# Cross-attention of the second layer: dividing by the softmax sum before the output projection, and projecting once per batch row instead of once per pair of heads

## What is computed

```python
x = x + tanh(g_xattn[0]) * xattn0(layernorm(x), ctx)     # 16 heads of 16
x = x + tanh(g_ffn[0])   * moe(layernorm(x))             # 16 experts
x = x + tanh(g_xattn[1]) * xattn1(layernorm(x), ctx)     # 16 heads of 128
x = x + tanh(g_ffn[1])   * ternary_ffn(layernorm(x))

def xattn1(t, c):                                        # the part that is changed
    q = (t @ Wq), k = (c @ Wk), v = (c @ Wv)             # two heads share a k and a v
    attn = softmax(mask(q @ k.T / sqrt(128)))            # (4, 16, 256, 1601)
    return (attn @ v).reshape(4, 256, 2048) @ Wo
```

## Time and profile before

| | us |
|---|---|
| median of 3 runs | 1572.19 (1567.17 to 1576.84) |
| the profiled execution | 1572.19, span of its instructions 1570.9 |
| mean granted TensorE clock in it | 0.962 of full speed |

### The profile page before, as it was taken

One profiled execution on the slowest core, in us unless ns is written; L12 is line 12 of the kernel. 1 busy time (PEld: TensorE's weight loads), 2 busy tenths in 40 slices (PEclk: granted clock), 3 DMA queues, 4 the chain that ended last, 5 costly groups with the idle time before them and its releaser, 6 DMA issues.

```text
span 1570.9 us, 25673 instructions
## 1 busy us (share of the span) xinstructions
PE 1378.6 (88%) x8430; PEld 682.5 (43%) x8524; DVE 1248.3 (79%) x2335; ACT 1106.1 (70%) x2028; POOL 780.8 (50%) x664
## 2 busy tenths in 40 slices
PE   5688798887887888789889989899998999999989
PEld 4243243343333234234445544455454545454545
DVE  5666667677677445769998888989899899999887
ACT  4656665864864665568778878778877787887764
POOL 4014013213213013238777658887697776676763
PEclk9798898999998999999999999999999999999999
DMA  4001300200242010010000000000010000000000
GB/s 165 1 1 29 58 1 1 50 15 1 43 129 83 2 54 1 6 43 22 6 1 1 1 22 22 7 1 22 1 27 1 28 3 26 10 19 1 1 1 28
DMA packets 20491, 36.71 MB, mean 23 GB/s; under 512 B 4898, under 2 KB 15238, under 8 KB 19334
## 3 DMA queue, kind: packets, MB, share of 16 engines
q1 hardware_dynamic: 20358, 35.07, 7.7%
HBM read 26.53 MB, written 1.15 MB: 18 GB/s over the span
## 4 chain that ended last, share of the span: by engine, by line
PE 33%; DVE 9%; issue 8%; POOL 4%; ACT 3%; DMA 0%; DVEq 0%; ACTq 0%; POOLq 0%
PE BK L713 32%; DVE arena L1696 4%; POOL arena L2092 3%; DVE arena L1677 2%; ACT arena L1954 1%; DVE arena L1710 1%; ACT arena L1947 1%; ACT arena L1965 0%; DVE arena L2280 0%; ACT L1947 0%; POOL arena L2089 0%; DMA arena<-in_wup 0%; POOL arena L1087 0%; DVE arena L998 0%; DVE arena L2286 0%
## 5 line engine op out<-in xcount | busy, mean ns | idle before, releaser
L713 PE MATMUL BK<-arena 128*128 128x512 bf16 (+12 forms) x8100 | 1332.5, 366 | 156.2 <-DVE arena L1514 40.9
L713 PEld LDWEIGHTS BK<-arena 128*128 128x128 bf16 (+6 forms) x8194 | 645.7, 110 | 812.5 <-issue 167.9
L2092 POOL TENSOR_TENSOR arena<-arena 128x512 f32<-128x512 f32 (+1 forms) x352 | 509.7, 1448 | 133.8 <-ACT arena L1947 108.9
L1696 DVE TENSOR_TENSOR arena<-arena 128x512 bf16<-128x512 f32 (+1 forms) x416 | 485.7, 1171 | 29.3 <-ACT arena L1954 28.2
L1947 ACT ACTIVATE arena<-BK,arena 128x512 f32<-128x512 f32 (+1 forms) x416 | 286.2, 688 | 125.2 <-PE BK L713 105.3
L1845 ACT ACTIVATE arena<-BK 128x512 f32<-128x512 f32 (+1 forms) x416 | 227.1, 603 | 97.2 <-PE BK L713 91.8
L1514 DVE TENSOR_REDUCE arena<-BK 128x1 f32<-128x512 f32 x384 | 244.5, 684 | 60.9 <-PE BK L713 59.9
L1954 ACT CAST arena<-arena 128x512 bf16<-128x512 f32 (+1 forms) x416 | 253.6, 610 | 0.0
L1677 DVE CUSTOM_DVE_ANT_0 arena<-BK,arena 128x512 bf16<-128x512 f32 (+1 forms) x256 | 145.3, 568 | 23.7 <-PE BK L713 21.1
L1965 ACT ACTIVATE arena<-BK 128x512 bf16<-128x512 f32 (+1 forms) x256 | 129.5, 508 | 45.5 <-PE BK L713 44.3
L2003 POOL TENSOR_TENSOR arena<-arena 128x256 f32<-128x256 f32 (+6 forms) x45 | 30.2, 670 | 188.1 <-ACT arena L1782 185.8
(11 more groups left out here) (178 smaller groups left out, 857.8 us busy)
## 6 DMA issues: line engine op xcount, KB each, us to landing
arena<-arena SPq DMA_DIRECT2D x144, 50.0 KB, 2.2
arena<-in_ctxT SPq DMA_DIRECT2D x8, 800.5 KB, 4.3
arena<-in_ctxk SPq DMA_DIRECT2D x4, 768.0 KB
arena<-in_wo SPq DMA_DIRECT2D x1, 2048.0 KB, 7.6
arena<-in_wqT SPq DMA_DIRECT2D x1, 2048.0 KB, 8.9
arena<-in_x SPq DMA_DIRECT2D x4, 256.0 KB, 9.9
arena<-in_rsel SPq DMA_DIRECT2D x1, 1024.0 KB, 9.6
arena<-in_rw1T SPq DMA_DIRECT2D x1, 1024.0 KB, 5.2
```

Of the source, the lines that this page charges most:

```text
L713: return T.matmul(out_, lhsT, rhs, start=start, stop=stop, skip_group_check=True)
L1696: V.tensor_tensor(Pl[k][0:m, :], P1[k][0:m, :], Ph[k][0:m, :], ALU.subtract).then_inc(p_low, 1)
L2092: G.tensor_tensor(acc[0:m, g % 2, :], acc[0:m, g % 2, :], P1[k][0:m, :], ALU.add).then_inc(summed1, 1)
```

## The change

The inverse of the softmax sum is multiplied in before the projection, and the projection is made per batch row. For each group GpSimd builds `dg`, four 128x128 diagonal matrices with the inverse sums on them (512 columns of f32). TensorE multiplies a matrix of ones with it, one f32 matmul of 512 columns (`o1b`): every partition of bank 7 then has the row of 512 inverse sums. ScalarE copies it to `rc`, VectorE multiplies the bank of `v1` by `rc` into `oN` (`o1c`). ScalarE's copy `o1v` is gone. `o1p` is no longer made per group: after groups 7, 15 and 23 it is two pieces, one for each 128 tokens, in which 16 heads are added up in PSUM by 16 f32 matmuls of 256 columns, followed by one VectorE addition to `x_sb` that also has the gate. For the last batch row the first 14 heads of both pieces (`o1h`) are put into `finish(31)`, around `o1b`.

```diff
         def finish(g):
             last = g == NG - 1
-            piece("o1v", g)
             piece("o1a", g, bank=7)
             yield
             yield
             if last:
                 piece("xh", 0)
-            for j in range(2):
-                piece("o1p", g, j, bank=4 + j if last else 7)
-                yield
+                self.fill(4, "o1p", B - 1, 0)
+                piece("o1h", 0)
+            piece("o1b", g, bank=7)
+            yield
+            if last:
+                self.fill(5, "o1p", B - 1, 1)
+                piece("o1h", 1)
+            piece("o1c", g)
+            yield
+            if g % 8 == 7:
+                for t in range(2):
+                    piece("o1p", g // 8, t, bank=None if last else 7)
+                    yield
...
+        def project1(i, t2, lo, hi):
+            for h in range(lo, hi):
+                t = mm(BK[i][:, 0:256], oN[:, h, 128 * t2:128 * t2 + 128], N1[:, h, :], start=(h == 0), stop=(h == H - 1))
+            return t
...
+                elif kind == "o1b":
+                    g, = arg
+                    pe.wait_ge(diag_done, g + 1)
+                    mm(BK[7][:, :], ones[:, :], dg[:, :, :].rearrange("p u n -> p (u n)")).then_inc(full[7], 1)
+                elif kind == "o1h":
+                    t2, = arg
+                    i, n = slot["o1p", B - 1, t2]
+                    pe.wait_ge(free[i], n)
+                    pe.wait_ge(pv_taken, 8 * B - 1)
+                    project1(i, t2, 0, H - 2)
                 elif kind == "o1p":
-                    g, j = arg
-                    h = 2 * (g % 8) + j
-                    pe.wait_ge(pv_taken, g + 1)
-                    for t2 in range(2):
-                        t = mm(BK[i][:, 256 * t2:256 * t2 + 256], oN[:, h, 128 * t2:128 * t2 + 128], N1[:, h, :])
-                    t.then_inc(full[i], 1)
+                    b, t2 = arg
+                    pe.wait_ge(pv_taken, 8 * b + 8)
+                    project1(i, t2, H - 2 if b == B - 1 else 0, H).then_inc(full[i], 1)
...
+                elif kind == "o1c":
+                    g, = arg
+                    h = 2 * (g % 8)
+                    j = 2 + g % 2
+                    dve.wait_ge(*emptied("o1b", g))
+                    dve.wait_ge(pv_done, 13 * (g + 1))
+                    if g >= 8:
+                        dve.wait_ge(*filled("o1p", g // 8 - 1, 1))
+                    V.tensor_tensor(oN[:, h:h + 2, :].rearrange("p h n -> p (h n)"), BK[j][:, :], rc[:, :],
+                                    ALU.mult).then_inc(pv_taken, 1)
                 elif kind == "o1p":
-                    g, j = arg
+                    b, t2 = arg
+                    k = 2 * b + t2
                     dve.wait_ge(full[i], n + 1)
-                    dve.wait_ge(gated, g + 1)
-                    if g:
-                        dve.wait_ge(*emptied("o1p", g - (j == 0), 1 - j))
-                    for t2 in range(2):
-                        k, u = 2 * (g // 8) + t2, 2 * j + t2
-                        t = V.scalar_tensor_tensor(out=x_sb[:, k, :], in0=BK[i][:, 256 * t2:256 * t2 + 256],
-                                                   scalar=dn[:, 8 + u:9 + u], in1=x_sb[:, k, :], op0=ALU.mult, op1=ALU.add)
-                    t.then_inc(free[i], 1)
+                    V.scalar_tensor_tensor(out=x_sb[:, k, :], in0=BK[i][:, 0:256], scalar=tg[:, 1:2], in1=x_sb[:, k, :],
+                                           op0=ALU.mult, op1=ALU.add).then_inc(free[i], 1)
...
-                elif kind == "o1v":
+                elif kind == "o1b":
                     g, = arg
-                    h, j = 2 * (g % 8), 2 + g % 2
-                    act.wait_ge(pv_done, 13 * (g + 1))
-                    if g >= 8:
-                        act.wait_ge(*filled("o1p", g - 8, 1))
-                    A.copy(oN[:, h:h + 2, :].rearrange("p h n -> p (h n)"), BK[j][:, :]).then_inc(pv_taken, 1)
+                    act.wait_ge(full[7], n + 1)
+                    act.wait_ge(pv_taken, g)
+                    A.copy(rc[:, :], BK[7][:, :]).then_inc(free[7], 1)
...
                     pool.wait_ge(dn_recip, g + 1)
                     if g:
-                        pool.wait_ge(*emptied("o1p", g - 1, 1))
-                    G.tensor_tensor(dn[:, 8:12], dn[:, 4:8], tg[:, 1:2].to_broadcast([128, 4]), ALU.mult).then_inc(gated, 1)
+                        pool.wait_ge(*filled("o1b", g - 1))
+                    G.tensor_tensor(dg[:, :, :], idn[:, :].unsqueeze(1).to_broadcast([128, 4, 128]),
+                                    dn[:, 4:8].unsqueeze(2).to_broadcast([128, 4, 128]), ALU.mult).then_inc(diag_done, 1)
```

More of the change, by code:

```diff
@@ L844, in program @@
         ones = sb("ones", [128, 128], F32, CTb)
-        dn = sb("dn", [128, 12], F32, CTb)
+        dn = sb("dn", [128, 8], F32, CTb)
         mng = sb("mng", [4, 2, 128], BF16, CTb)
@@ L852, in program @@
         acc = sb("acc", [128, 2, 512], F32, L1)
+        dg = sb("dg", [128, 4, 128], F32, SM)
+        rc = sb("rc", [128, 512], F32, L1)
         oN = sb("oN", [128, H, S], F32, L1)
@@ L981, in dve_norm_stats @@
                 else:
-                    dve.wait_ge(*emptied("o1p", 8 * b + 7, 1))
+                    dve.wait_ge(*emptied("o1p", b, i % 2))
                 V.bn_stats(bns[:, i, :], x_sb[:, i, :]).then_inc(dve_chain.sem, dve_chain.up())
@@ L1095, in program @@
         ac_done = sem("ac_done")
-        mcb_done, q_high, max1_done, p_high, p_low, summed1, pv_done, gated, ck_high, ck_low, tern_done = (
+        mcb_done, q_high, max1_done, p_high, p_low, summed1, pv_done, diag_done, ck_high, ck_low, tern_done = (
             sem(n) for n in ("mcb_done", "q_high", "max1_done", "p_high", "p_low", "summed1", "pv_done",
-                             "gated", "ck_high", "ck_low", "tern_done"))
+                             "diag_done", "ck_high", "ck_low", "tern_done"))
         l1_set, t_lt, t_half, dn_recip, pv_taken = (sem(n) for n in ("l1_set", "t_lt", "t_half", "dn_recip", "pv_taken"))
```

## The result

| | before | after |
|---|---|---|
| median, us | 1574.51 (1567.17 to 1579.65, 4 runs) | 1623.64 (1619.86 to 1627.32, 4 runs) |
| profiled execution, us | 1572.19 | 1623.28 |
| mean granted TensorE clock | 0.962 | 0.960 |

The changed kernel is slower: 1.032 of the time before, 95% interval 1.029 to 1.036. The forecast was 1598, so 26 of the 51 us between the two profiled executions were foreseen.

The account below looks back on a forecast made before the run. The prediction took single attention groups as bound by TensorE (plain) or by VectorE or GpSimd (side work). From 1572.2 us, -24.4 + 11 - 4.8 + 33 + 11.5 = +26.3 gave 1598 us, range 1581 to 1616.

Parts of the forecast that it names:

- the old wait for `L1710`: TensorE's wait for VectorE's addition to free bank 7 between a group's two projection pieces would go: -4.8 us.
- wait before `o1b`: TensorE waits for GpSimd's diagonals in ten groups where GpSimd is late: +11 us, bounds 0 and 18.5.
- three bursts: Groups 8, 16 and 24 each get a batch row's projection, 13.8 us of matmuls: +33 us, bounds +26 and +39.
- end: After the last `v1`, more matmuls stand exposed before the norm's transposes: +11.5 us, bounds 10 and 12.
- 28 x -0.87: Groups 1 to 31 without 8, 16 and 24 each gain 0.87 us, whether TensorE or VectorE holds them: -24.4 us.
- the norm's transposes waiting for `L998`: Credit within the bursts: the transposes move a group later and no longer wait for line 998, -4.6 us.
- near 38 us: Sign of being right: length of batch rows' first groups, with two runs of f32 matmuls of 6.9 us each.
- GpSimd's price for VectorE: In each group, 0.85 us more GpSimd stretches VectorE's subtractions by 0.36 us per us, 0.3 us.
- all 0.85 us lost: Hardest reading of the SBUF lock: VectorE's relief falls from 0.9 to 0.36 us in 19 groups, 10 us more.
- VectorE is the bound: Rival: VectorE bounds the stage, TensorE has room; 28 groups gain 1.21 us each, 1572 us, not slower; chance 0.18.
- The waits are swallowed: Rival: late groups have slack, so the wait before `o1b` costs +2 and the bursts +28: 1584 us; chance 0.17.
- The wait is the main cost: Rival: stalls before `o1b` cost 18.5 us, halve the clock twice, and VectorE's gain is lost: 1616 us; chance 0.15.

Follow-up runs that it names:

- e4: The kernel before plus one f32 matmul of 512 columns with ones in each group, result overwritten; 1594.02 us, 1.013.
- e2: The changed kernel with `o1b` and what follows it two tiles later, except in groups 7, 15, 23 and 31; 1614.20 us, 1.026.
- e8: The kernel before with two of VectorE's four additions of a group left out, 0.95 us a group; 1574.18 us, 0.999.
- e15: The changed kernel with projection per group, no bursts, `o1b` two tiles and projection one tile later except in each batch row's last group; 1590.91 us, 1.014.
- e12: The changed kernel with diagonals made by ScalarE instead of GpSimd, and diagonals and ones in bf16; 1626.24 us, 1.034.
- e13: e2 with diagonals and ones in bf16, so that `o1b` takes 0.22 instead of 0.86 us; 1607.41 us, 1.023.
- e7: The changed kernel with diagonals and ones in bf16, so that `o1b` takes 0.22 instead of 0.86 us; 1622.61 us, 1.032.
- e11: The kernel before with one more tile between the two projections of a group, no work changed; 1567.77 us, 0.996.
- e3: e2 with GpSimd's product cut from 512 columns to 4 and the diagonals set to ones; 1606.92 us, 1.021.
- e10: The kernel before plus GpSimd's product of 512 columns in each group, its result unused; 1582.62 us, 1.006.
- e5: The changed kernel without diagonals: a matmul of ones with the sums, and VectorE inverts 512 columns instead of four; 1679.11 us, 1.067.

## Why the direction was right and the size was not

The sum by its own terms, with what the runs showed:

| term | forecast | measured | by |
|---|---|---|---|
| matmul with ones, 0.86 in a plain group | 0.86 | 0.86 | e4 |
| plain group | -0.87 | -0.89 | after |
| 28 groups, without the new wait, and the old wait for `L1710` | -24.4 - 4.8 = -29.2 | -7.1 (712.2 to 705.1) | e2 |
| wait before `o1b` | +11 | +11.8 (705.1 to 716.9) | e2 and after |
| three bursts | +33 | +36.5 | after |
| end | +11.5 | +11.4 | after |

**The step that failed is "28 x -0.87".** I priced groups that TensorE fills by TensorE and the 19 others by VectorE, at 0.9 each, and called the one gain "as good as" the other. The first half holds in the five plainest groups: 24.04 us came to 23.15. The second does not: e8 took 0.95 us of VectorE out of every group and the time did not move, and e15 against e2 shows that TensorE's own time isn't the price there either. Group by group, e2 against before (one profile each): the 19 gave -2.5 us in all, between -2.4 and +3.3 each, where -16.5 was booked for them and -4.8 for the old wait; the nine that TensorE fills gave -4.6 of their -7.8, mostly since group 9, the first behind a burst, became 1.7 longer. These two differences, 18.8 and 3.2, are the distance from -29.2 to -7.1, and with 3.5 us of the bursts nearly all that the forecast missed.

**Why the others don't give it back.** Over groups 9 to 15 of e2 no engine is full: TensorE 92%, VectorE 89%, GpSimd 83%. What holds such groups, by my reading, are handovers: a tile needs ScalarE's exponential and cast, VectorE's subtraction and then TensorE, each in its fixed order, and each can be late at another place. Much of what leaves TensorE becomes idle time there (36.3 us in the stage of e15, 60.9 in e2), and the largest of its waits, for the subtraction, grew (20.6 to 36.0 us in the stage). Two further signs: TensorE's work put in costs 0.7 us for each (e4, in part perhaps the clock), taken out it gives half (e12), a third of it in the 28 groups (e15 to e2), a quarter (e13) or nothing (e7); and e11, which takes out no work at all, gains 6 us. Which handover limits which group wasn't settled, and that it is handovers is not shown either; the experiments show that it is neither VectorE's work nor TensorE's alone, and that GpSimd's is worth a quarter of its time (e3, e10).

**The credits for waits that vanish.** I booked the old wait for `L1710` as -4.8. e11 shows that this wait is worth as much when it is removed and nothing else is changed. In after it was replaced: the waits for the subtraction rose by 7.8 us. The 4.6 us of the norm's transposes waiting for `L998` did leave groups 8 and 24, but the transposes went to groups 9, 17 and 25, and there they wait 4.6 us for line 1711 to have read bank 7. So this credit was spent in the 28 groups: the three behind a burst came out 2.4 us longer in after, where 2.6 less was forecast. The bursts themselves came out at +36.5, within their bounds of 26 to 39: of the four terms between 38.8 and 33 only the half clock in group 8, which did go, can be seen by itself, and the wait of 1.2 us for ScalarE that I put in each is not among the waits of after. That ScalarE and VectorE stand through a burst was right. The sign "near 38 us" did not fit the sum, whose +33 on 88.3 makes 40.4 a group; measured were 44.8, 39.9 and 40.1.

**The wait before `o1b`.** 16.3 us against 18.5 worked out from the late starts of GpSimd, nine times against ten; it cost 9.5 to 11.8 of that. Each of the nine is within 0.2 us of its forecast; the tenth, in group 17 behind a burst, is missing. Reading from a four-column operation how late a queue is, and adding what a longer one takes, worked. The product took 1.41 to 1.49 us in the stage, as the nearest row said. That the 11 comes so near is in part luck: it was a choice between 0 and 18.5.

**GpSimd's price for VectorE.** I read 0.36 us of stretched subtractions for each us of GpSimd off and the earlier trace rows. In e10 35.5 us more of GpSimd made the subtractions 1.4 us longer, in e3 32 us less made them 5 us shorter. So this term of 0.3 was too large, and the reading "all 0.85 us lost" falls with it; since VectorE's relief is worth nothing, neither changes the sum.

**The rivals.** "VectorE is the bound" falls with e8. "The waits are swallowed" falls with e2. "The wait is the main cost" gave 1616, nearest to the 1624; two of its parts came true, the clock drops behind stalls of 3.4 us (three behind this wait, two were put in) and VectorE's gain lost in its groups, but its name did not: with the wait gone 1.026 is left. The forecast with two of its terms changed, VectorE's relief at nothing and the old wait not gained, is 1598 + 16.5 + 4.8 = 1619. The first stood in the text as a bound (+16). The bounds all together ended at +57, 1629, and would have held the 1624; the range was taken from the rivals instead and ended at 1616, where it holds that one bound and nothing beside it. No row had spoken for the 0.9 but the stretching of the subtractions, which shows that instructions stand and not what follows from it.

From the kernel before to the one after, in steps that runs separate: the division ahead of the projection, with its matmul with ones, +21 (e15), the projections moved into bursts and the end +20 (e2 against e15), `o1b` before its diagonals are ready +9.5 (after against e2); 51 together. That the first step is the matmul's time is argued from e4, which has the matmul alone and the same ratio.

## What to carry to other kernels

Price work taken from an engine only in stretches where that engine is full, and at far less elsewhere (here from nothing to a half), however close the shares of two engines are; work put in cost most of its length (0.7 in e4). Work that is moved from where it is partly hidden into one uninterrupted run costs its whole length there, since in-order engines that wait for its result prepare nothing. Before merging or moving work, look for the small waits that a different place in the order removes: one empty step between two uses of the same PSUM bank gained 0.4% where this change lost 3.2%.

## What the runs showed of the hardware

- VectorE's reciprocal of 128x512 f32 takes 3.34 us, 6.5 ns a column, against 0.18 us for 128x4; a multiplication of the same size from PSUM takes 0.68. The Trainium skill (VectorE: DVE Perf Modes, "First, the fixed hardware budget") says that it is done by an iterated division with a repeat count of 8, which fits a price per column of this kind, though no run here shows how it is made.
- Leaving 62 instructions out of VectorE's order (29 us) took 12 us off its busy time; the 416 subtractions with both inputs in SBUF took 10 us more, 1195 ns instead of 1171 in the mean (e8). Busy time of such an engine isn't work alone.
- 35.5 us more of GpSimd's products in the stage left the mean of the same subtractions at 1174 ns (1171 before), and the kernel became 9 us longer (e10).
- A stall of TensorE of 3.36 us was followed by 3.4 us at a granted clock of 0.50 (1.2 of 2.4 GHz). The profiles of before, after, e7 and e5 have 3.4, 13.7, 37.5 and 75.1 us at that level in the stage. A stall of 2.55 us was followed by the same in after and not in before. The Trainium skill (TensorE: Matmul & The Clock Gate, "Why this matters for your kernels") warns of idle gaps between bursts of matmuls; the rows of after agree.
